# Two-layer transformer block on one core: the first layer's bias adds placed right behind the norms, its fourth turn three steps later, and the scaling of the second layer's down weights cut in four

## The chip, the cores and the metric

The kernel runs on one core of one Trainium2 chip. The metric is the device time of one execution in microseconds (us), the median of several runs. The profile is of one further execution, recorded instruction by instruction.

## The reference

`x` is 2 x 1024 tokens of width 256, in 32-bit floats. Two layers follow one another, each `x = x + attention(norm(x)) + ffn(norm(x))`:

```
xn = layernorm(x)                                   # layer 0
q, k, v = xn @ W.T + b ; qp, kp = elu(q)+1, elu(k)+1
kv = kp^T v ; z = qp . sum(kp)
attention0 = (qp @ kv) / (z + eps) @ o_w.T + o_b    # 16 heads, linear attention
ffn0 = (silu(xn @ U.T) * (xn @ G.T)) @ D.T          # ternary weights, 256 -> 1024 -> 256
xn = layernorm(x)                                   # layer 1
attention1 = softmax attention with rotary positions, 16 heads, @ out_w.T + out_b
ffn1: Walsh-Hadamard transforms around a gated FFN; its last product is scaled by Wscale_dp per output column
```

What matters here: `o_b` is a row of 256 numbers that is added to every token of `x`. `Wscale_dp` is a row of 256 numbers that scales the columns of layer 1's down weights, and a Hadamard transform of those weights over 1024 is folded into them before they are used.

## The kernel before

One function, `work_order`, writes out a single list of pieces (`put("kv_in", 3, bank)`). Each engine walks that list and issues, for every piece whose name it has a function for, its own part of it, so the list is every engine's order at once, and an engine never starts a later piece before an earlier one. Semaphores order the engines among each other.

Tokens are in four chunks of 512 (four tiles of 128). The stages around the change are these.

- **Norms.** For chunk n: `ln_stats` (VectorE statistics, then `rstd` to the power -1/2 on GpSimd), `ln_norm` (VectorE writes the normed chunk XC from X, four operations, line 1144 of the profile), `ln_turn` (TensorE transposes it, line 807; ScalarE copies the high part XH, line 1437; VectorE forms the low part XL, line 1150). X itself is only read.
- **bias.** `bias(0, c)` is one GpSimd operation, 128 x 1024, that adds `o_b` (the tile OB) to chunk c of X (line 1601). It may run once `ln_norm` has read the chunk. VectorE's later additions into X wait for it, and `load_ob1`, the load of the second layer's row into OB, waits for all four.
- **The linear attention (`attention0`, drawn as `side0`).** `kv_in(tt)` projects one tile (TensorE), VectorE adds the biases into zk and ve (lines 1215, 1216), ScalarE computes ek (lines 1454, 1456), and `kv_sum(tt)` on VectorE joins zk and ek, both in SBUF (line 1235). `kv_out` multiplies. `q0(c, m)` does the queries: QP on VectorE (line 1230), zs on ScalarE (lines 1466, 1468), the sum on GpSimd (line 1613). `att_n`, `att_t`, `att_b` apply the attention. `att_n(8)` is the first of the second batch and waits for `q0(2, 1)`.
- **Ternary weights.** `tern_abs` sums the absolute values of a 1 MB weight on ScalarE (line 1446), `tern_scale` and `tern_cut` cut it on VectorE: one operation over 2048 columns (line 1178) and two over 1024 with two SBUF inputs (line 1186). TU and TG are the up and gate weights, TD the down weights.
- **The first FFN (`main(0)`, from "half" on), woven with the rest of `side0`.** `gate`: TensorE, ScalarE's tanh (line 1508), VectorE (line 1267). `up`: TensorE, VectorE (line 1280), ScalarE's copy hh (line 1516), GpSimd's low part hl (line 1646). `down`: TensorE (line 775).
- **Second layer's down weights, on GpSimd.** `fold` multiplies the staged 128 x 2048 weights by the row WSD (line 1607). Then six `butterfly` operations of 128 x 1024 (line 1622), and `load_up` loads the next weights over them. They are put at steps of `side0`: fold at step 18, butterflies at steps 19, 22, 25, 28, 31 and 34.

Around the first norms the list before reads: `ln_norm 2`, `kv_in 1`, `kv_sum 0`, `kv_in 2`, `kv_sum 1`, `ln_turn 2`, `tern_scale 0`, `kv_in 3`, `kv_sum 2`, `ln_stats 3`, `tern_cut 0 0`, `kv_out 0`, `q0 0 0`, `ln_norm 3`, `tern_cut 0 1`, `q0 0 1`, `ln_turn 3`, `tern_abs 1`, `kv_in 4`, `kv_sum 3`, `kv_out 1`, `kv_in 5`, `kv_sum 4`, `tern_scale 1`, `kv_out 2`, `kv_in 6`, `kv_sum 5`, `tern_cut 1 0`, `kv_out 3`, `kv_in 7`, `kv_sum 6`, `tern_cut 1 1`, `kv_out 4`, `q0 1 0`, `bias 0 0`, `tern_abs 2`, `q0 1 1`, `bias 0 1`, `kv_sum 7`, `kv_out 5` to `7`, `kv_sums 0`, `bias 0 2`, `att_n 0`, `bias 0 3`, and then the FFN.

Of the kernel before, what the change touches and what calls it, by code (L numbers as in the profile page):

```python
# [8 lines left out]
ALU = mybir.AluOpType  # L9
# [40 lines left out]
class Ring:  # L50
# [5 lines left out]
    def next(self):  # L56
        self.i = (self.i + 1) % len(self.slots)
        return self.slots[self.i]
# [12 lines left out]
def work_order():  # L71
# [3 lines left out]
    def put(*piece):  # L75
        order.append(piece)
# [64 lines left out]
    def attention0():  # L141
        for tt in range(8):
            yield from kv(tt)
            if tt % 4 == 3:
                for m in range(2):
                    yield from q0(tt // 4, m)
        yield from kv_end(0)
        for h in range(4):
            yield from att_n(2 * h)
            if h:  # L150
                yield from att_b(h - 1)
            yield from att_n(2 * h + 1)
            yield from kv(8 + 2 * h)
            yield from att_t(h)
            yield from kv(9 + 2 * h)
        yield from q0(2, 0)
        yield from att_b(3)
        yield from q0(2, 1)
        yield from kv_end(1)
        for h in range(4, 8):  # L160
            yield from att_n(2 * h)
            if h > 4:
                yield from att_b(h - 1)
            yield from att_n(2 * h + 1)
            if h < 6:
                yield from q0(3, h - 4)
            else:
                yield
            yield from att_t(h)
            yield  # L170
        yield from att_b(7)
# [40 lines left out]
    def qk(c, n, count):  # L212
        put("qk", c, n, ps.next(), ps.next())
        yield
        for k in range(count):
            yield
            if k == 0:
                put("qk_join", c, n)
        put("qk_split", c, n)

    def side0():
        bf = 0
        for n, _ in enumerate(attention0()):
            if 14 <= n < 18:
                next(tn)
                if n == 17:
                    put("scales")
                    put("spread_vb")
                    put("load_wa1")
            if n == 18:  # L230
                put("fold")
            if n == 30:
                put("add_vb", ps.next())
            if n >= 18 and n % 3 == 1 and bf < 6:
                put("butterfly", bf)
                bf += 1
                if bf == 6:
                    put("load_up")
            yield
        ps.slots.append(2)  # L240
        put("prep_attn1")
        put("load_gate")
        put("difference", 0)
        yield
        for q in range(4):
            put("prep_down", q, ps.next())
            yield
            if q == 0:
                put("total", 0)
            if q == 1:  # L250
                put("difference", 1)
            if q == 3:
                put("total", 1)
        for u in range(8):
            put("prep_ug", u, ps.next())
            yield
            if u == 1:
                put("low_attn1", 0)
            if u == 5:
                put("low_attn1", 1)  # L260
        for c in (0, 1):
            for n in range(2):
                yield from qk(c, n, 4)
        put("load_m", 0)
        put("load_m", 1)
# [26 lines left out]
    next(tn)  # L292
    put("signs")
    sd0 = side0()
    next(sd0)
    next(ln0[2])
    next(sd0)
    for n in range(FIRST):
        if n < 10:
            next(tn)  # L300
        next(sd0)
        if n < 4:
            next(ln0[2 if n == 0 else 3])
        if n > 7:
            put("bias", 0, n - 8)
    put("half")
    put("load_down")
    put("load_ob1")
# [85 lines left out]
    while s < 8 * NP + LAG or any(k >= s for k in plan):  # L394
        live = s < 8 * NP
        for piece in plan.get(s, []):
            if piece[0] == "recip":
                p = piece[1]
# [23 lines left out]
        if 0 <= s - LAG < 8 * NP:  # L422
# [4 lines left out]
            elif t % 8 == 7:  # L427
                p = t // 8
# [18 lines left out]
def program(nc, x_d, wa0, tern, wa1, wo1, wf1, cols_d, bkv_d, cos_d, sin_d, had_d, mask_d, ident_d, pad_d, sel_d, wl_d, ob_d, wsd_d, y_d):  # L447
    with ExitStack() as ctx:
        base = -(-nc.sbuf_base // 32) * 32

        def sb(name, kb, shape, dt=F32):
            return nc.alloc_sbuf_tensor_at(name, shape, dt, offset=base + int(kb * KB))

        q = {n: ctx.enter_context(nc.semaphore(f"s_{n}")) for n in SEMAPHORES}
        d = {n: ctx.enter_context(nc.semaphore(f"d_{n}")) for n in DMAS}
# [46 lines left out]
        stg = [sb(f"stg{i}", 174 + 8 * i, [128, 2048]) for i in range(2)]  # L502
# [7 lines left out]
        WSD = sb("WSD", 203, [128, 256])  # L510
# [54 lines left out]
        def over_tiles(row, n):  # L565
            return row[:, :].rearrange("p (o d) -> p o d", o=1).broadcast_to([128, n, 256])
# [16 lines left out]
        def o_slots(p):  # L583
# [7 lines left out]
            return (f"oe{o}", n), (f"num{i}", done), (f"rc{o}", n), (f"rs{o}", n)  # L591

        order = work_order()
        block = ctx.enter_context(nc.Block())

# [989 lines left out]
        def _(e):  # L1585
# [14 lines left out]
                    e.wait_ge(q["ob"], 1)  # L1600
                e.tensor_tensor(xs, xs, over_tiles(OB, 4), ALU.add).then_inc(q["bx"], 1)

            def fold():
                raw = stg[0][:, :].rearrange("p (o d) -> p o d", d=256)
                e.wait_ge(d["st0"], STAGE["down"][1])
                e.wait_ge(d["wsd"], 16)
                e.tensor_tensor(raw, raw, over_tiles(WSD, 8), ALU.mult).then_inc(q["fold"], 1)

            def q0(c, m, b):
                i = 2 * c + m  # L1610
# [3 lines left out]

            def butterfly(k):
                if k == 0:
                    e.wait_ge(q["fold"], 1)
                elif k % 2 == 0:
                    e.wait_ge(q["bf"], k)
                pair = (stg[0][:, :], stg2[:, :])  # L1620
                a, z = (x.rearrange("p (o t i) -> p o t i", t=2, i=256 << k // 2) for x in (pair if k // 2 % 2 == 0 else pair[::-1]))
                e.tensor_tensor(z[:, :, k % 2, :], a[:, :, 0, :], a[:, :, 1, :], ALU.subtract if k % 2 else ALU.add).then_inc(q["bf"], 1)
# [84 lines left out]
            def low(g):  # L1707
# [3 lines left out]
                if g == 2:  # L1711
# [4 lines left out]
                    e.wait_ge(q["fill"], 2)  # L1716

            parts = {f.__name__: f for f in (ln_stats, bias, fold, q0, butterfly, low_attn1, difference, total, up, hidden, ones_v, qk_join, load_wl, out, recip, times, high, low)}
            for name, *args in order:
                if name in parts:  # L1720
# [84 lines left out]
```

## Time and profile before

| | |
|---|---|
| median of 3 runs | 731.92 us (730.15 to 731.93) |
| the profiled execution | 732.69 us, of it 730.9 us from first to last instruction |
| TensorE busy | 699.4 us (96%) |
| VectorE, ScalarE, GpSimd busy | 529.2, 432.9, 288.2 us |
| mean granted TensorE clock | 0.986 of full speed |

An operation's start and duration are on one line of the timeline, with the idle time of its engine before it and what ended that in brackets. A duration runs from issue to end, so an operation that stands waiting inside its engine shows as a long one. Neighbouring operations of an engine overlap by some hundredths of a microsecond.

### The profile page before, as it was taken

How to read it: one execution, taken by the hardware profiler on the slowest of the kernel's cores; microseconds unless marked ns; L12 is line 12 of the kernel's file. 1: busy time of each engine (PE TensorE's matmuls, PEld its weight loads, DVE VectorE, ACT ScalarE, POOL GpSimd, SP SyncE). 2: the span in 40 equal slices, each digit the busy share in tenths (PEclk: the TensorE clock that was granted, in tenths of full speed). 3: DMA queues.
4: the chain of work that ended last, by engine and by line, in shares of the span. 5: the costliest groups of instructions: out<-in, count | busy, mean ns of one | idle time of the engine just before them, and what ended most of it. 6: DMA issues, size and time to landing. Idle time of an engine off the chain costs nothing.

```text
span 730.9 us, 11063 instructions
## 1 busy us (share of the span) xinstructions
PE 699.4 (96%) x4246; PEld 441.5 (60%) x4246; DVE 529.2 (72%) x864; ACT 432.9 (59%) x592; POOL 288.2 (39%) x261
## 2 busy tenths in 40 slices
PE   7787999989998999999999999999999999999998
PEld 6576898977776888677676773333333333333445
DVE  7878875655668677678778788888886388888315
ACT  3363434446543522432332338999998999999883
POOL 2237944348665632542543431122333224332410
PEclk8999999989999999999999999999999999999999
DMA  7157001012025562423111022344443344433321
GB/s 266 55 187 231 1 1 58 1 26 91 1 87 173 167 208 87 144 70 105 59 59 35 25 67 71 126 140 160 123 143 126 100 146 146 145 94 91 105 79 58
DMA packets 25848, 74.14 MB, mean 101 GB/s; under 512 B 4620, under 2 KB 5996, under 8 KB 24964
## 3 DMA queue, kind: packets, MB, share of 16 engines
q1 hardware_dynamic: 21268, 65.37, 26.9%
q0 software_dynamic: 3808, 7.60, 3.6%
q8 instruction: 34, 0.56, 0.3%
q10 hardware_dynamic: 720, 0.48, 0.2%
q14 instruction: 18, 0.15, 0.1%
HBM read 54.54 MB, written 23.06 MB: 106 GB/s over the span
## 4 chain that ended last, share of the span: by engine, by line
PE 78%; DVE 10%; issue 5%; ACT 4%; POOL 3%; DMA 1%; DVEq 0%; ACTq 0%; POOLq 0%
PE PS L769 22%; PE PS L1038 17%; PE PS L1024 12%; PE PS L775 12%; PE PS L1007 6%; PE PS L997 5%; DVE mx L1342 1%; DVE bst L1128 1%; PE PS L903 1%; PE PS L858 1%; POOL hl L1646 1%; DVE sg L1280 1%; DVE rot L1325 1%; ACT XD L1432 1%; DMA X<-in_x 1%
## 5 line engine op out<-in xcount | busy, mean ns | idle before, releaser
L1554 ACT ACTIVATE P<-PS 128x1024 f32<-128x1024 f32 x256 | 249.0, 1024 | 30.0 <-PE PS L1024 29.7
L1349 DVE TENSOR_REDUCE mx<-PS 128x1 f32<-128x512 f32 x300 | 189.1, 682 | 32.3 <-PE PS L1007 30.6
L1342 DVE TENSOR_REDUCE mx<-PS 128x2 f32<-128x1024 f32 x106 | 124.8, 1220 | 36.6 <-PE PS L997 36.3
L1038 PE MATMUL PS<-P,VV 128*32 128x512 f32 x1024 | 136.4, 605 | 0.1
L1646 POOL TENSOR_TENSOR hl<-sg,hh 128x512 fp32r<-128x512 f32 x64 | 85.2, 1332 | 126.1 <-ACT hh L1524 75.8
L1024 PEld LDWEIGHTS PS<-QS,KS 64*128 64x128 f32 x512 | 48.4, 183 | 121.3 <-ACT P L1554 109.5
L1024 PE MATMUL PS<-QS,KS 64*128 64x512 f32 x512 | 116.4, 455 | 0.9 <-DVE mx L1342 0.6
L1007 PE MATMUL PS<-KM,QM 64*128 64x512 f32 x300 | 81.0, 395 | 0.0
L1510 ACT ACTIVATE sg<-PS,cols 128x512 f32<-128x512 f32 x32 | 22.0, 688 | 86.9 <-PE PS L769 86.9
L769 PE MATMUL PS<-XH,UGH 128*128 128x512 f32 x128 | 54.4, 425 | 3.7 <-DVE sg L1278 2.0
L769 PE MATMUL PS<-XL,UGH 128*128 128x512 f32 x128 | 50.5, 394 | 0.0
L769 PE MATMUL PS<-XH,UGL 128*128 128x512 f32 x128 | 50.0, 391 | 0.0
L1516 ACT ACTIVATE hh<-sg 128x512 fp32r<-128x512 f32 x32 | 20.1, 630 | 49.3 <-DVE sg L1280 49.3
L1655 POOL TENSOR_TENSOR sg<-sg,us 128x512 f32<-128x512 f32 x24 | 30.9, 1286 | 35.7 <-ACT us L1519 35.7
L1038 PEld LDWEIGHTS PS<-P,VV 128*32 128x32 f32 x1024 | 20.2, 108 | 39.8 <-issue 35.3
L997 PE MATMUL PS<-KM,QM 64*128 64x512 f32 x212 | 39.9, 448 | 0.8 <-DVE mx L1342 0.6
L1007 PEld LDWEIGHTS PS<-KM,QM 64*128 64x128 f32 x300 | 38.0, 185 | 3.4 <-DVE mx L1349 0.6
L775 PE MATMUL PS<-DH,hh 128*128 128x256 f32 x128 | 38.0, 297 | 0.0
L775 PE MATMUL PS<-DL,hh 128*128 128x256 f32 x128 | 36.1, 282 | 0.0
L775 PE MATMUL PS<-DH,hl 128*128 128x256 f32 x128 | 36.1, 282 | 0.0
L769 PEld LDWEIGHTS PS<-XH,UGH 128*128 128x128 f32 x128 | 24.0, 188 | 19.6 <-issue 10.8
L775 PE MATMUL PS<-TD,hh 128*128 128x256 f32 x128 | 34.0, 300 | 1.6 <-POOL hl L1646 1.6
(212 smaller groups left out, 1358.6 us busy)
## 6 DMA issues: line engine op xcount, KB each, us to landing
QM<-scr_q SPq DMA_DIRECT2D x16, 512.0 KB, 4.3
KM<-scr_k SPq DMA_DIRECT2D x16, 512.0 KB, 5.3
QS<-scr_q SPq DMA_DIRECT2D x16, 512.0 KB, 4.5
KS<-scr_k SPq DMA_DIRECT2D x16, 512.0 KB, 5.4
scr_q<-spl SPq DMA_DIRECT2D x24, 256.0 KB, 3.2
scr_k<-spl SPq DMA_DIRECT2D x24, 256.0 KB, 3.4
scr_o<-OE POOLq DMA_DIRECT2D x14, 256.0 KB, 2.8
stg<-in_tern SPq DMA_DIRECT2D x3, 1024.0 KB, 6.1
```

The costliest lines, as they stand in the source:

```text
L769: i = e.matmul(out, l, r, start=start and j == 0, stop=stop and j == len(pairs) - 1)
L775: i = e.matmul(out[:, r * 256:r * 256 + 256], l, x, start=first and r == 0 and j == 0, stop=last and j == len(pairs) - 1, skip_group_check ...
L997: e.matmul(bank[b + h], QM[p % 2][hr, qt * 128:(qt + 1) * 128], KM[p % 2][hr, chunk(half)], start=True, stop=True).then_inc(q["mt"], 1)
L1007: e.matmul(bank[b], QM[p % 2][hr, qt * 128:(qt + 1) * 128], KM[p % 2][hr, chunk(half)], start=True, stop=True).then_inc(q["mt"], 1)
L1024: i = e.matmul(bank[b + h], KS[p % 2][hr, kt * 128:(kt + 1) * 128], QS[p % 2][hr, chunk(half)], start=True, stop=True)
L1038: i = e.matmul(PS[32 * c:32 * c + 32, 7, :], v_head(8 * b + kt, 2 * j + c // 2), P[s % 4][:, chunk(c // 2 + 2 * (c % 2))], start=(kt == 0) ...
L1342: e.tensor_reduce(mx[p % 2][:, :, qt, half], PS[:, b:b + 2, :], AX.X, ALU.max).then_inc(q["mx"], 2)
L1349: e.tensor_reduce(mx[p % 2][:, h, qt, half:half + 1], bank[b], AX.X, ALU.max).then_inc(q["mx"], 1)
L1510: e.activation(s[:, :], bank[b], ACT.Silu, scale=col("wsg", m) if layer else su).then_inc(q["t"], 1)
L1554: e.activation(P[s % 4][:, half * 1024:(half + 1) * 1024], PS[:, b:b + 2, :].rearrange("p b n -> p (b n)"), ACT.Exp).then_inc(q["ex"], 1)
L1646: e.tensor_tensor(hl[f % 4][:, :], sg[f % 3][:, :], r32(hh[f % 4][:, :]), ALU.subtract).then_inc(q["hl"], 1)
L1655: e.tensor_tensor(s[:, :], s[:, :], us[f % 4][:, :], ALU.mult).then_inc(q["h"], 1)
```

## The change

The first three bias adds stand right behind `ln_norm 2` and before `kv_in 1`; the fourth stands behind `ln_norm 3`. `ln_turn 3` moves from step 3 of the loop to step 6, that is behind `kv_in 6` and `kv_sum 5`. `fold` becomes four operations over 512 columns, at steps 18 to 21 of `side0`. The six butterflies begin at step 22 instead of 19, so they stand at steps 22, 25, 28, 31, 34 and 37, and `load_up` with the last.

```diff
-            if n == 18:
-                put("fold")
+            if 18 <= n < 22:
+                put("fold", n - 18)
             if n == 30:
                 put("add_vb", ps.next())
-            if n >= 18 and n % 3 == 1 and bf < 6:
+            if n >= 22 and n % 3 == 1 and bf < 6:
                 put("butterfly", bf)
...
     next(ln0[2])
+    for c in range(3):
+        put("bias", 0, c)
     next(sd0)
     for n in range(FIRST):
         if n < 10:
             next(tn)
         next(sd0)
-        if n < 4:
+        if n in (0, 1, 2, 6):
             next(ln0[2 if n == 0 else 3])
-        if n > 7:
-            put("bias", 0, n - 8)
+        if n == 2:
+            put("bias", 0, 3)
...
-            def fold():
-                raw = stg[0][:, :].rearrange("p (o d) -> p o d", d=256)
+            def fold(k):
+
+                raw = stg[0][:, 512 * k:512 * k + 512].rearrange("p (o d) -> p o d", d=256)
                 e.wait_ge(d["st0"], STAGE["down"][1])
                 e.wait_ge(d["wsd"], 16)
-                e.tensor_tensor(raw, raw, over_tiles(WSD, 8), ALU.mult).then_inc(q["fold"], 1)
+                e.tensor_tensor(raw, raw, over_tiles(WSD, 2), ALU.mult).then_inc(q["fold"], 1)
...
-                    e.wait_ge(q["fold"], 1)
+                    e.wait_ge(q["fold"], 4)
```

## Rows read from the trace of the kernel before

**Rows 1.** The page: busy time by engine, and shares of the chain that ended last.
```profile
PE 699.4 (96%) x4246; PEld 441.5 (60%) x4246; DVE 529.2 (72%) x864; ACT 432.9 (59%) x592; POOL 288.2 (39%) x261
...
PE 78%; DVE 10%; issue 5%; ACT 4%; POOL 3%; DMA 1%; DVEq 0%; ACTq 0%; POOLq 0%
```

**Rows 2.** Two stretches: length, busy time of each engine, clock, DMA share, GB/s.
```profile
50.00:72.00 22.00, 17.19 (x84) 13.70 (x82) 16.60 (x35) 9.19 (x16) 18.16 (x10) 0.92 0.83 284
72.00:118.00 46.00, 45.82 (x279) 41.04 (x280) 34.16 (x64) 19.54 (x36) 31.54 (x17) 1.00 0.07 25
```

**Rows 3.** Timeline of TensorE: four operations that begin after idle time.
```profile
33.53 1.21 PE L807 MATMUL PS<-IDN,XC 128*128 128x128 f32 x7 [3.20 <-DVE XC L1144]
...
65.76 0.80 PE L769 MATMUL PS<-XH,TG 128*128 128x512 f32 x1 [1.96 <-DVE sg L1267]
...
72.18 0.73 PE L858 MATMUL PS<-kvb,QP 128*128 128x136 f32 x4 [1.42 <-DVE at L1247]
...
119.71 0.70 PE L858 MATMUL PS<-kvb,QP 128*128 128x136 f32 x4 [0.47 <-POOL QP L1613]
```

**Rows 4.** Timeline of GpSimd from 14 to 120 us.
```profile
15.03 2.98 POOL L1592 TENSOR_TENSOR rstd<-rstd,MINUS_HALF 128x4 f32<-128x4 f32 x1 [4.62 <-DVE rstd L1135]
...
51.10 2.40 POOL L1601 TENSOR_TENSOR X<-X,OB 128x1024 f32<-128x1024 f32 x1
...
54.70 8.10 POOL L1601 TENSOR_TENSOR X<-X,OB 128x1024 f32<-128x1024 f32 x3
62.77 3.48 POOL L1646 TENSOR_TENSOR hl<-sg,hh 128x512 fp32r<-128x512 f32 x2
...
71.32 4.60 POOL L1607 TENSOR_TENSOR stg<-stg,WSD 128x2048 f32<-128x2048 f32 x1
...
80.93 2.40 POOL L1622 TENSOR_TENSOR stg<-stg 128x1024 f32<-128x1024 f32 x1
...
116.68 1.54 POOL L1646 TENSOR_TENSOR hl<-sg,hh 128x512 fp32r<-128x512 f32 x1 [1.21 <-ACT hh L1516]
118.28 1.28 POOL L1613 TENSOR_TENSOR QP<-zs,QP 128x512 f32<-128x512 f32 x1
```

**Rows 5.** Timeline of VectorE from 57 to 82 us.
```profile
57.93 2.62 DVE L1178 TENSOR_SCALAR TD<-stg,s 128x2048 fp32r<-128x2048 f32 x1
...
62.94 2.17 DVE L1186 SCALAR_TENSOR_TENSOR TD<-stg,s,TD 128x1024 fp32r<-128x1024 f32 x1
...
66.63 1.27 DVE L1186 SCALAR_TENSOR_TENSOR TD<-stg,s,TD 128x1024 fp32r<-128x1024 f32 x1
...
81.11 2.50 DVE L1235 SCALAR_TENSOR_TENSOR zk<-zk,ek 128x256 f32<-128x256 f32 x1
```

**Rows 6.** Timeline of VectorE from 20 to 44 us.
```profile
20.91 1.37 DVE L1144 TENSOR_SCALAR XC<-X,mv,rstd 128x256 f32<-128x256 f32 x4
...
22.87 0.41 DVE L1235 SCALAR_TENSOR_TENSOR zk<-zk,ek 128x256 f32<-128x256 f32 x1
...
25.03 1.29 DVE L1150 TENSOR_TENSOR XL<-PS,XH 128x512 fp32r<-128x512 f32 x2 [0.75 <-ACT XH L1437]
...
38.11 1.29 DVE L1150 TENSOR_TENSOR XL<-PS,XH 128x512 fp32r<-128x512 f32 x2 [1.90 <-ACT XH L1437]
...
42.02 1.29 DVE L1178 TENSOR_SCALAR TG<-stg,s 128x2048 fp32r<-128x2048 f32 x1
```

**Rows 7.** Timeline of ScalarE from 24 to 39 us.
```profile
24.42 1.07 ACT L1437 ACTIVATE XH<-PS 128x512 fp32r<-128x512 f32 x2
...
38.45 1.91 ACT L1446 ACTIVATE TG<-stg 128x2048 fp32r<-128x2048 f32 x1
```

**Rows 8.** Slices of one microsecond, columns as in rows 2: the granted clock.
```profile
34.00:35.00 1.00, 1.00 (x7) 0.71 (x6) 1.00 (x3) 0.12 (x1) 0.74 (x1) 0.90 0.00 0
...
38.00:39.00 1.00, 1.00 (x6) 0.88 (x5) 0.89 (x2) 1.00 (x3) 1.00 (x1) 0.89 1.02 434
65.00:66.00 1.00, 0.24 (x1) 0.24 (x2) 1.00 (x4) 0.00 (x0) 1.00 (x1) 0.76 0.29 84
...
71.00:72.00 1.00, 0.00 (x0) 0.00 (x0) 0.93 (x4) 0.00 (x0) 1.00 (x2) 1.00 0.91 365
```

## Prediction

> **What bounds the kernel now.** I read the page first, then the chain that ended last, then the stages, then the engines' timelines. The page says TensorE: 96% busy, 78% of the chain [rows 1]. That is an average. The edits all touch work before 120 us, and there two stages differ. From 72 to 118 us TensorE is busy 45.8 of 46 us: whatever only moves GpSimd or VectorE there costs nothing. From 50 to 72 it is busy 17.2 of 22 and VectorE 16.6 [rows 2]. The idle times say who is waited for: TensorE waits 3.20 us for the fourth norm, 1.96 for VectorE's `sg`, 1.42 for VectorE's `at`, and, in the otherwise full stage, 0.47 us for GpSimd's `QP` [rows 3]. So the start is a chain through VectorE with ScalarE between, and a microsecond lost or won before the full stage reaches the end whole, since nothing behind it runs to a clock of its own.
>
> The second thing to see is that VectorE and GpSimd hold each other up. The cut of TD over 2048 columns took 2.62 us at 57.93, while three biases ran from 54.70; the same operation on TG, with GpSimd idle, took 1.29 [rows 4, 5, 6]. The cut over 1024 took 2.17 beside an `hl` and 1.27 alone. A `kv_sum` took 2.50 when a butterfly had begun 0.18 us before it, and 0.41 elsewhere [rows 4, 5, 6]. It is mutual: the `rstd` at 15.03 took 2.98 us [rows 4]. The pairs read as a queue of one: whoever comes second stands until the other's running operation ends, then gets its turn. The two `hl` at 62.77 show the turn-taking: 3.48 us for two, with the cut's 1.1 us between them [rows 4, 5].
>
> **Part 1, the first three biases early.** GpSimd is free at 15.03 + 2.98 = 18.01 us. A bias takes 2.40 us, about 2.35 from start to start [rows 4]. Biases 0 and 1 fill 18.0 to 22.7. Bias 2 needs the third norm, which ends at 20.91 + 1.37 = 22.28, so it runs from 22.7 to 25.05. `kv_sum 0`, with two SBUF inputs, comes at 22.87 [rows 6], 0.17 us after it, and waits to 25.05: **+2.2 us**. Behind it on VectorE stand `kv_in 2`, `kv_sum 1` and the third turn's XL; ScalarE's ek and XH hang on `kv_in 2`, so the 0.75 us of idle before XL at 25.03 [rows 6] gives nothing back, as XH comes from behind ek [rows 7]. VectorE is nearly unbroken from there to the fourth norm, and the whole chain moves by 2.2. Bounds: 0.9, if `kv_sum 0` wins and `kv_sum 1` at 23.87 waits instead, and 2.2. I take 2.2, since the pair 0.18 us apart lost too [rows 4, 5].
>
> The norms themselves (line 1144) I cost at nothing beside the biases: 256 columns in 0.34 us is half the rate of the cut, 2048 in 1.29 [rows 6], so this form does not run at the double rate at which the cut was held up. The Trainium skill ("VectorE: DVE Perf Modes", section "What auto-detection actually checks") would have a one-source operation with source and result in SBUF and even dimensions use both ports, and so be locked out by GpSimd; by that the norm would wait for bias 1 as well, some 1.4 us more than my sum. The trace's rate for this line speaks against it.
>
> **Part 2, the fourth bias and the fourth turn.** Today VectorE idles 1.90 us before the fourth turn's XL at 38.11 [rows 6], because transposes and XH come first. ScalarE's sum over TG begins at 38.45, right behind that XH pair (as long as the pair at 24.42, 1.07 us) [rows 7]. With the turn behind `kv_sum 5`, the sum over TG no longer waits for XH: -1.05 us, on top of +2.2. VectorE's `kv_sum 3` then meets bias 3, and `kv_sum 4` the `QP` sum behind it; the first hides under the wait for ScalarE, the second I put at +0.45 (bounds 0 and 1.3, one such operation). So the TG cut now at 42.02 starts 2.2 - 1.05 + 0.45 = 1.6 later. From there VectorE has no gap to the FFN, and XL's 1.2 us (1.29 [rows 6] less overlap) now stands in it, with 0.8 us of idle ahead, as before the third turn's XL, which follows `kv_in` and `kv_sum` in just this order: 0.75 [rows 6]. **The FFN starts 1.6 + 2.0 = 3.6 us later**; with every bound low 0.9 - 1.05 + 0 + 1.2 = 1.05, with all high 4.5.
>
> **Part 3, GpSimd free from 50 to 63 us.** The cut at 57.93 loses its wait, 2.62 - 1.29 = 1.33; the cut at 62.94 loses 2.17 - 1.27 = 0.9, as the first `hl` is then long done and the second ends as the cut begins [rows 5, 6]. Both lie on the chain through `sg` to TensorE's starts at 65.76 and 72.18 [rows 3]. **-2.2 us** (bounds -2.2, and -1.3 if the second `hl` still meets the cut).
>
> **Part 4, TensorE's clock.** It fell to its half level, 1.2 GHz, twice. It fell at 34.9 after 3.2 us of idle and came back at 38.1; it fell at 65.7 after idle 0.66 and 1.96 us with a small product between, and came back near 69. After 1.4 us of idle, at 71 to 72, it held [rows 3, 8]. Both low stretches lie where VectorE sets the pace, and cost nothing today. In the new order the up product now at 65.76 comes 2.2 earlier and at full clock; what follows it up to the wait for `at` is done 3.7 us earlier, but that wait ends only 2.2 earlier, so idle grows from 1.4 to about 3 us. The nearest row is the 3.2. If the clock falls there, its low stretch of about 3.3 us lies in the full stage, where it costs half its length: **+1.6** (bounds 0 and 1.6).
>
> **Part 5, fold and butterflies.** Four folds of 512 columns cost at most four `hl`, 4 x 1.25 = 5.0 us, for 4.60 now [rows 4]; four `hl` fit between them. All of it lies under TensorE's full stage [rows 2]; without that cover the 0.4 us would show. But the last butterfly moves to step 37, which is behind `hl` of `up 0 1 2` and ahead of the `hl` and the `QP` sum for which `att_n 8` waits. GpSimd is free at 116.68 - 1.21 = 115.47. A butterfly of 2.40 ends at 117.87, the waiting `kv_sum 15` takes 0.35, `hl` 1.25, the sum 1.28: 120.8 instead of 119.56. TensorE already waits there [rows 3, 4]: **+1.2 us** (bounds 0 and 1.25). `load_up` goes out some 9 us later and has over 40 us left. SP's queue gains: `load_ob1` no longer waits long for the biases, and nothing behind it was late.
>
> **Sum.** 3.6 - 2.2 + 1.6 + 1.2 = +4.2 us. Against the profiled execution, 732.69 + 4.2 = 736.9; the median of the runs is 0.77 lower, so 736.1. All bounds low: 1.05 - 2.2 = -1.15, or 730.8. All high: 4.5 - 1.3 + 1.6 + 1.25 = 6.05, or 738.
>
> **Rivals.**
> - *The clock holds* at the 3 us gap: +2.6, 734.5. For it: two levels, one switch, and only two falls to judge by.
> - *`kv_sum 0` slips in before bias 2*: 1.3 less, 734.8 or, with the clock held, 733.2. It is decided by 0.17 us.
> - *The early cost is absorbed.* VectorE's 1.90 us of idle at 38.11 [rows 6] takes up most of the 2.2, and TensorE's 0.47 is all that `att_n 8` shows: start +1.5, then -2.2, then +0.5: no change, 731.7. Against it: the idle goes only if TG's sum comes earlier, and that hangs on the same chain.
> - *Faster: TensorE, not VectorE, ends the chain from 33 to 49 us.* Then the moved turn fills its 3.20 us of idle [rows 3] with `kv_in 4`, the low stretch there is gone (-1.6), TG's sum gives its 1.05, and with -2.2 and +1.2 this is -3.65: 728.3. It decides from the point where the TG cut starts before about 41 us. Against it: `kv_in 4`'s bank is freed by `q0 0 0`, which hangs on VectorE.
> - *The norm is locked out too*: +1.4, 737.5. In a sentence apart, this is the rule of the Trainium skill named above.
>
> **How the numbers follow.** A measurement here tells about 0.3%, 2.2 us, from no change. The forecast at 736.1 gets 0.30 (its own range 735 to 737), the clock held 0.20, `kv_sum 0` first 0.14 (0.08 of it slower), absorbed 0.21, faster 0.13, norm locked out 0.02. Slower 0.30 + 0.20 + 0.08 + 0.02 = 0.60; same 0.06 + 0.21 = 0.27; faster 0.13. The range 731 to 738 leaves out the faster case and little above.
>
> **What would show it.** Right: `kv_sum 0` with over 2 us in it; the TG cut near 43.6 and 1.29 long; XL of the fourth turn with idle before it; gate's first tanh near 56.4 (52.8 now); the TD cut 1.29 long; a low clock just behind 72 us; `att_n 8` waiting over 1 us for `QP`. Wrong: biases beside a short `kv_sum 0`, or a TG cut at or before 42 us.

## The result, and the profile after

The changed kernel took 738.59 us (median of 4, 737.02 to 739.1) beside 731.92 (median of 4): ratio 1.0091, 95% interval 1.0070 to 1.0111. It is slower, as forecast, by 6.7 us where 4.2 was forecast, and 0.6 us above the stated range. The same kernel measured once more, in another group (run f1 below), took 737.3 beside 732.0: ratio 1.0079 (1.0059 to 1.0098). The profiled execution took 737.02 us, span 735.1: 4.3 above the profiled execution of before. That the profiled spans and the forecast both say +4.2 is luck; the part on the prediction works it out.

The first place to look is where the two traces part. In the timeline of VectorE before, lines that stand in no group above (the first four are the small operations of the piece `signs`, which prepares constants):

```profile
18.25 0.16 DVE L1163 TENSOR_SCALAR s<-cols 128x2 f32<-128x2 f32 x1
18.32 0.16 DVE L1164 TENSOR_SCALAR s16b<-cols 128x8 f32<-128x8 f32 x1
18.39 0.16 DVE L1165 TENSOR_SCALAR MINUS_QB<-cols 128x2 f32<-128x2 f32 x1
18.46 0.16 DVE L1167 TENSOR_SCALAR MASK<-MASK 128x8 f32<-128x8 f32 x1
20.24 0.42 DVE L1215 TENSOR_TENSOR zk<-PS,BKV 128x256 f32<-128x256 f32 x1 [1.61 <-PE PS L769]
...
23.20 0.42 DVE L1215 TENSOR_TENSOR zk<-PS,BKV 128x256 f32<-128x256 f32 x1
```

The timeline of VectorE after (line numbers are two higher, and three behind the fold on GpSimd):

```profile
18.04 2.14 DVE L1165 TENSOR_SCALAR s<-cols 128x2 f32<-128x2 f32 x1
20.09 0.16 DVE L1166 TENSOR_SCALAR s16b<-cols 128x8 f32<-128x8 f32 x1
20.16 2.31 DVE L1167 TENSOR_SCALAR MINUS_QB<-cols 128x2 f32<-128x2 f32 x1
22.39 0.16 DVE L1169 TENSOR_SCALAR MASK<-MASK 128x8 f32<-128x8 f32 x1
22.47 0.41 DVE L1217 TENSOR_TENSOR zk<-PS,BKV 128x256 f32<-128x256 f32 x1
...
23.13 1.37 DVE L1146 TENSOR_SCALAR XC<-X,mv,rstd 128x256 f32<-128x256 f32 x4
...
25.09 2.14 DVE L1237 SCALAR_TENSOR_TENSOR zk<-zk,ek 128x256 f32<-128x256 f32 x1
27.15 0.41 DVE L1217 TENSOR_TENSOR zk<-PS,BKV 128x256 f32<-128x256 f32 x1
...
41.09 2.17 DVE L1237 SCALAR_TENSOR_TENSOR zk<-zk,ek 128x256 f32<-128x256 f32 x1
...
45.08 1.29 DVE L1180 TENSOR_SCALAR TG<-stg,s 128x2048 fp32r<-128x2048 f32 x1
...
48.12 1.29 DVE L1152 TENSOR_TENSOR XL<-PS,XH 128x512 fp32r<-128x512 f32 x2 [0.76 <-ACT XH L1439]
...
63.04 1.29 DVE L1180 TENSOR_SCALAR TD<-stg,s 128x2048 fp32r<-128x2048 f32 x1
...
66.71 1.33 DVE L1188 SCALAR_TENSOR_TENSOR TD<-stg,s,TD 128x1024 fp32r<-128x1024 f32 x1
...
119.62 1.42 DVE L1237 SCALAR_TENSOR_TENSOR zk<-zk,ek 128x256 f32<-128x256 f32 x1
```

The timeline of GpSimd after, beside [rows 4]:

```profile
17.76 4.69 POOL L1603 TENSOR_TENSOR X<-X,OB 128x1024 f32<-128x1024 f32 x2
24.58 2.37 POOL L1603 TENSOR_TENSOR X<-X,OB 128x1024 f32<-128x1024 f32 x1 [2.13 <-DVE XC L1146]
...
118.37 2.38 POOL L1625 TENSOR_TENSOR stg<-stg 128x1024 f32<-128x1024 f32 x1
120.72 1.46 POOL L1649 TENSOR_TENSOR hl<-sg,hh 128x512 fp32r<-128x512 f32 x1
122.13 1.27 POOL L1616 TENSOR_TENSOR QP<-zs,QP 128x512 f32<-128x512 f32 x1
```

TensorE after, the two starts that answer to the last two of [rows 3], and ScalarE's first tanh, which was at 52.77 before:

```profile
75.12 0.73 PE L860 MATMUL PS<-kvb,QP 128*128 128x136 f32 x4 [2.84 <-DVE at L1249]
...
123.55 0.70 PE L860 MATMUL PS<-kvb,QP 128*128 128x136 f32 x4 [0.73 <-POOL QP L1616]
```

```profile
57.88 0.67 ACT L1510 ACTIVATE sg<-PS,s 128x512 f32<-128x512 f32 x1
```

Read as a ledger of one event after another against its old time: `kv_in 0` on VectorE +2.2 (22.47 for 20.24); `kv_in 2` +4.0 (27.15 for 23.20); the TG cut +3.1; the first tanh +5.1; `att_n 3` on TensorE +2.9; `att_n 8` +3.8; the end +4.2. The forecast had 3.6, 1.4, 4.2 (with the clock) for the tanh, `att_n 3` without the clock, and the end. Most of the distance from the forecast is made before 28 us: 4.0 at `kv_in 2`, where 2.2 was forecast, and 1.5 more than forecast at the tanh and at `att_n 3`. Two operations over two columns each, which need 0.16 us each, stand 2.14 and 2.31 us behind biases 0 and 1. The prediction charged nothing for them.

### The profile page after: what moved, and what is told of

It reads as the page before. It is cut to its first block, busy times and chain, and to the rows that moved or that the text cites. A ratio compares the mean times of both kernels' runs of the same rounds, so it can differ in the third digit from the quotient of the medians.

```text
span 735.1 us, 11069 instructions
## 1 busy us (share of the span) xinstructions
PE 702.2 (96%) x4246; PEld 443.8 (60%) x4246; DVE 534.4 (73%) x864; ACT 433.0 (59%) x592; POOL 286.8 (39%) x264
## 4 chain that ended last, share of the span: by engine, by line
PE 75%; DVE 12%; issue 5%; ACT 4%; POOL 3%; DMA 1%; DVEq 0%; ACTq 0%; POOLq 0%
PE PS L771 20%; PE PS L1040 17%; PE PS L1026 12%; PE PS L777 11%; PE PS L1009 6%; PE PS L999 5%; DVE bst L1130 1%; DVE mx L1344 1%; PE PS L905 1%; PE PS L860 1%; DVE sg L1282 1%; DVE XL L1152 1%; POOL hl L1649 1%; DVE rot L1327 1%; ACT XD L1434 1%
## 5 line engine op out<-in xcount | busy, mean ns | idle before, releaser
L1518 ACT ACTIVATE hh<-sg 128x512 fp32r<-128x512 f32 x32 | 20.2, 630 | 47.2 <-DVE sg L1282 47.2
L1040 PEld LDWEIGHTS PS<-P,VV 128*32 128x32 f32 x1024 | 20.2, 108 | 39.7 <-issue 35.2
```

The lines of the kernel that those rows point to most:

```text
L1040: i = e.matmul(PS[32 * c:32 * c + 32, 7, :], v_head(8 * b + kt, 2 * j + c // 2), P[s % 4][:, chunk(c // 2 + 2 * (c % 2))], start=(kt == 0) ...
```

## The experiments

Each kernel was run in several rounds beside the kernel before. The medians of before in the three groups (a, e and f) were 732.07, 731.67 and 732.0. A difference in us behind a ratio is that ratio times 732.

**a3, only the biases.** The kernel before with

```diff
     next(ln0[2])
+    for c in range(3):
+        put("bias", 0, c)
     next(sd0)
...
-        if n > 7:
-            put("bias", 0, n - 8)
+        if n == 2:
+            put("bias", 0, 3)
```

> The kernel before with only the four bias adds moved; turn, fold and butterflies stay. Theory A, the early biases are the loss: VectorE's two 128x2 operations of the signs piece stand 2.1 and 2.3 us and kv_sum 0 another 2.1, in all about 3.9 us before the FFN starts, and 2.2 come back at the cuts of TD: slower by 1.5 to 2.5 us. Theory B, the moved turn is the loss: within 1 us of the kernel before, or faster.

734.98 us, ratio 1.0038 (1.0023 to 1.0052): +2.8, somewhat above the 1.5 to 2.5 expected. The two small operations again took 2.14 and 2.31 us and `kv_sum 0` 2.15. In its trace `att_n 3` comes at 74.18, 2.0 later than before. Against the second measurement of the changed kernel, +5.3, the early biases alone make about half of the loss.

**a1, only the fourth turn.**

```diff
-        if n < 4:
+        if n in (0, 1, 2, 6):
             next(ln0[2 if n == 0 else 3])
```

> The kernel before with only the fourth turn moved to step 6. Theory A: the cut of TG starts about 1 us earlier, then XL with 0.8 us of idle adds 2.0: the FFN starts 1 us later, slower by 0.5 to 1.5 us. Theory B: slower by over 2 us. A third view, that TensorE sets the pace there: faster by 1 us or more.

731.99 us, ratio 1.0002 (0.9991 to 1.0013). The expected +0.5 to +1.5 is not in the median, though the interval, up to +1.0, leaves room for its lower half. The traces do show it at the stage's end: beside a2, whose early order is that of before and whose `kv_in 0` reached VectorE at the same time (19.18 for a1's 19.20), the sum kvb comes 1.08 us later. First a1, then a2, timeline of VectorE:

```profile
50.26 0.44 DVE L1224 TENSOR_TENSOR kvb<-PS,MASK 128x272 f32<-128x272 f32 x1 [0.89 <-PE PS L841]
```

```profile
49.18 0.44 DVE L1224 TENSOR_TENSOR kvb<-PS,MASK 128x272 f32<-128x272 f32 x1 [0.89 <-PE PS L841]
```

Where that microsecond goes in the median is not settled. That a1's own sum is no later than that of before (50.26 for 50.23) has another reason: `kv_in 0` came a microsecond earlier in a1's trace, of which more in the section on the prediction.

**a2, only fold and butterflies.** The kernel before with the fold and butterfly edits of the change, nothing else.

> The kernel before with only fold in four and the butterflies three steps later. Both theories: att_n 8 waits for QP behind the last butterfly, +0.9 to +1.2 us, and nothing else; from 72 to 118 us no difference. Rival: the fold in four helps or hurts the hl behind it, then over 1.5 us either way.

732.55 us, ratio 1.0010 (0.9997 to 1.0022). In its trace TensorE waits 0.75 us for `QP` at `att_n 8` (0.47 before), and `kv_sum 15` takes 1.43. The expected +0.9 to +1.2 lies inside the interval, and so does no change.

**a4, the small operations out of the way.** The changed kernel with the three operations on `cols` put earlier on VectorE; the row of MASK stays where it was.

```diff
         next(ln0[i])
+    put("signs")
     put("w0h")
...
-    put("signs")
+    put("mask_row")
...
```

`mask_row` is the last operation of `signs`, now a piece of its own.

> The changed kernel with the three small operations of the signs piece put ahead of the low part of W0, before any bias can run; the mask row stays. Theory A: they take 0.16 us each, kv_in 0 ends at its old time, kv_sum 0 still stands 2.2 us: 1.7 to 2.4 us faster than the changed kernel. Rival: kv_in 0 was late for another reason (TensorE, the loads): no difference from the changed kernel, 737 to 739 us.

736.6 us, ratio 1.0058 (1.0042 to 1.0075): 2.0 faster than the first measurement of the changed kernel, 0.7 than the second. The traces show 0.5 (first tanh 57.40 for 57.88, `att_n 3` 74.63 for 75.12), not the 1.7 to 2.4 expected. The expectation was right about the operations and wrong about what comes behind them. Timeline of VectorE, then of GpSimd, of a4:

```profile
15.01 0.16 DVE L1168 TENSOR_SCALAR MINUS_QB<-cols 128x2 f32<-128x2 f32 x1
...
18.48 2.15 DVE L1172 TENSOR_SCALAR MASK<-MASK 128x8 f32<-128x8 f32 x1
20.54 0.41 DVE L1220 TENSOR_TENSOR zk<-PS,BKV 128x256 f32<-128x256 f32 x1
...
21.21 2.88 DVE L1147 TENSOR_SCALAR XC<-X,mv,rstd 128x256 f32<-128x256 f32 x4
...
24.67 2.12 DVE L1240 SCALAR_TENSOR_TENSOR zk<-zk,ek 128x256 f32<-128x256 f32 x1
```

```profile
18.20 4.76 POOL L1606 TENSOR_TENSOR X<-X,OB 128x1024 f32<-128x1024 f32 x2
24.16 2.35 POOL L1606 TENSOR_TENSOR X<-X,OB 128x1024 f32<-128x1024 f32 x1 [1.20 <-DVE XC L1147]
```

Now the MASK row stands 2.0 us behind bias 0, all but hidden under VectorE's wait for TensorE (`kv_in 0` at 20.54 for 20.24), and the norm, 1.37 us elsewhere, takes 2.88: it stands 1.5 us behind bias 1. This is the case to which the prediction gave 0.02. In the changed kernel the norm escapes only because the small operations had already spent that time: it starts at 23.13, after bias 1 ended at 22.45.

**e1, a fuller gap.** The changed kernel with products that nobody reads, in the gap before `att_n 3`:

```diff
     weave(main(0), sd0, RATE0)
+    k = order.index(("att_n", 3, 0))
+    order.insert(k, ("busy", 12, 4))
```

> The changed kernel with 12 more products of ones with ones on TensorE, into a free bank, in the idle time ahead of att_n 3 (added work, thrown away). Theory A, the clock falls behind that gap in most executions: 1.2 to 1.8 us faster than the changed kernel, about 737.0, and the granted clock at full level from 72 to 85 us. Rival, the clock is not it and the profiled execution was only a lucky one: no difference, or 0.5 us slower if the added products get in the way.

736.54 us, ratio 1.0070 (1.0053 to 1.0087). In its trace the products fill the gap (2.94 us), no idle time is left before `att_n 3`, and the clock stays full behind it. What that is worth is judged beside f1.

**f1, the changed kernel once more, and f2, e1 with 6 products in place of 12.**

> The changed kernel itself once more, beside the others of this group. If its first four runs were fair: 738 to 739. If they were on the unlucky side of the clock's falls: 737 to 738, and then the added products of e1 bought at most 0.5 us and biases with turn (e4) are within 1.5 us of the whole change.

> The changed kernel with 6 added products before att_n 3 instead of 12, so that they end well before the gap does (the 12 took 2.94 us of 2.84). Clock theory: 0.5 to 1.5 us faster than f1, since the gap is half filled. Rival, the falls only move elsewhere: the same as f1.

f1 took 737.3 us, ratio 1.0079; f2 736.73, ratio 1.0076 (1.0057 to 1.0094). The medians of e1 and f2 lie 0.8 and 0.6 below f1, well inside the intervals: no gain is shown. The two traces of the same kernel, though, price a fall of the clock. Slices of two microseconds behind `att_n 3`, the clock third from the right: first the changed kernel, then f1, the same code.

```profile
76.00:78.00 2.00, 2.00 (x10) 1.60 (x9) 1.48 (x5) 1.01 (x2) 1.60 (x2) 1.00 0.00 0
78.00:80.00 2.00, 2.00 (x15) 1.84 (x14) 1.89 (x5) 0.92 (x3) 2.00 (x2) 1.00 0.00 0
```

```profile
76.00:78.00 2.00, 2.00 (x6) 1.51 (x6) 1.10 (x4) 0.67 (x2) 1.52 (x2) 0.50 0.00 0
78.00:80.00 2.00, 2.00 (x8) 1.59 (x7) 0.84 (x2) 0.42 (x1) 2.00 (x2) 0.71 0.00 0
```

And TensorE's starts in f1:

```profile
75.20 0.79 PE L860 MATMUL PS<-kvb,QP 128*128 128x136 f32 x4 [2.84 <-DVE at L1249]
...
125.21 0.70 PE L860 MATMUL PS<-kvb,QP 128*128 128x136 f32 x4 [0.73 <-POOL QP L1616]
```

From `att_n 3` to `att_n 8` it is 48.43 us in the one and 50.01 in the other: 1.58 for one fall, after the same 2.84 us of idle. The low stretch lasts 3.4 us. The same idle time brought the fall in one execution and not in the other. Of the seven traces with that gap of 2.84 or 2.85 us, f1, f3, a3, a4 and e2 show the fall behind it, and the changed kernel's first trace and e4 don't. In f2 the products took 1.60 us, 1.19 us of idle stayed, and the clock held. What the products save there is not visible in the medians. One reason can be read from the traces: the clock is not settled behind `att_n 8` either. Around an idle time of 1.2 to 1.3 us, between 154 and 162 us, it fell in 12 of the 14 traces, and the time from `att_n 8` to the end differs with it: 608.8 and 609.2 us in e2 and f2, where it held; 610.0 to 611.1 in the ten with a low stretch of 3.4 us; 611.2 and 611.6 in before and the changed kernel's first trace, where it was low for 6.8. So f1 is 1.66 later than that first trace at `att_n 8` and 0.1 later at the end (735.2 for 735.1). One trace for each kernel can't say how often each case comes.

**e4, biases and turn without the fold part.** The changed kernel with fold and butterflies as before.

> The changed kernel with fold and butterflies as before: biases and turn moved. If the three parts add up, 735.0 + 0.1: near 735. If biases and turn make each other worse (bias 3 runs beside kv_sum 3 only when the turn is away), 737 to 738; the fold part is then worth 0.5 to 1 us.

736.15 us, ratio 1.0064 (1.0049 to 1.0079). Its first tanh comes at 57.91 and `att_n 3` at 75.14, as in the changed kernel (57.88, 75.12); `att_n 8` at 122.68, 0.87 earlier. Biases and turn together are worth +4.7, more than a3's 2.8 and a1's 0.2, though the intervals (3.6 to 5.8; 1.7 to 3.8; -0.7 to 1.0) allow them to add up. In the traces the turn adds 0.96 us to a3 (first tanh 56.95, here 57.91); for the rest of the difference I can name no wait.

**f3, the last butterfly at its old step.**

```diff
-            if n >= 22 and n % 3 == 1 and bf < 6:
+            if n in (22, 24, 26, 28, 31, 34):
```

> The changed kernel with the butterflies at steps 22, 24, 26, 28, 31 and 34, so the last stands where the last stood before. If part 5 is right, att_n 8 waits 0.5 us instead of 0.7, its product with kv_sum 15 is not held, and 0.6 to 1.0 us come back against f1. Rival: the denser butterflies hold up other kv_sums under TensorE's full stage, which shows as idle TensorE between 80 and 115 us: no gain.

735.08 us, ratio 1.0053 (1.0036 to 1.0071), 2.2 below f1 in the medians, where 0.6 to 1.0 was expected. Its trace has the clock fall of f1, so the two can be laid side by side:

```profile
124.31 0.70 PE L860 MATMUL PS<-kvb,QP 128*128 128x136 f32 x4 [0.47 <-POOL QP L1616]
```

124.31 for 125.21: the butterfly ahead of `QP` costs 0.90 us. The wait for `QP` itself grows only from 0.47 to 0.73; the rest is the product with `kv_sum 15`, which waited 0.39 us for VectorE, and the start behind it.

**e2, the biases in VectorE's gaps.** The kernel before, with turn and fold as before, and the biases where VectorE runs only operations that were never seen to wait for GpSimd: those with an input from PSUM, and a few small ones. Two of those, in the timeline of before, beside bias 0 (51.10 to 53.50) and bias 1 (from 54.70) of [rows 4]:

```profile
52.34 0.14 DVE L1199 TENSOR_SCALAR s<-s 128x1 f32<-128x1 f32 x1
...
55.07 0.25 DVE L1243 RECIPROCAL rz<-rz 128x16 f32<-128x16 f32 x1
```

The edit:

```diff
+        if n == 3:
+            put("bias", 0, 1)
         next(sd0)
+        if n == 0:
+            put("bias", 0, 0)
...
-        if n > 7:
-            put("bias", 0, n - 8)
+        if n in (8, 9):
+            put("bias", 0, n - 6)
...
+                if layer == 0 and c == 0:
+                    e.wait_ge(q["kvk"], 2)
+                if layer == 0 and c == 1:
+                    e.wait_ge(q["tt"], 2)
```

> The kernel before with the four bias adds where VectorE needs no second port: bias 0 after kv_sum 1, bias 1 after the first cuts of TU, biases 2 and 3 in the places of the old 0 and 1. Theory A, only the lockout makes early biases dear: nothing is lost before 50 us, the cuts of TD take 1.29 and 1.3, TensorE reaches att_n 3 2.2 us earlier, but the clock now falls in the full stage (+1.6): 0 to 1 us faster than before, 731 to 732. Rival, early biases cost through something else (the semaphores, GpSimd's rstd): slower than before.

729.92 us, ratio 0.9979 (0.9968 to 0.9990): faster than both kernels, 1.5 us below before, where 0 to 1 was expected. Timelines of GpSimd, VectorE and TensorE:

```profile
23.44 2.39 POOL L1609 TENSOR_TENSOR X<-X,OB 128x1024 f32<-128x1024 f32 x1 [5.56 <-issue]
...
35.68 2.39 POOL L1609 TENSOR_TENSOR X<-X,OB 128x1024 f32<-128x1024 f32 x1
...
50.14 2.40 POOL L1609 TENSOR_TENSOR X<-X,OB 128x1024 f32<-128x1024 f32 x1
...
53.75 2.41 POOL L1609 TENSOR_TENSOR X<-X,OB 128x1024 f32<-128x1024 f32 x1
```

```profile
56.98 1.50 DVE L1182 TENSOR_SCALAR TD<-stg,s 128x2048 fp32r<-128x2048 f32 x1
```

```profile
69.27 0.73 PE L862 MATMUL PS<-kvb,QP 128*128 128x136 f32 x4 [2.85 <-DVE at L1251]
```

From the TD cut to `att_n 3` it is 12.29 us (69.27 - 56.98), 14.25 before (72.18 - 57.93). (The cut takes 1.50, not 1.29: it began while an `hl` ran.) So the good half of the change, worth 2 us at `att_n 3`, can be had without its loss. The trace has the clock's fall behind `att_n 3`, which should take most of that back; why the median gains 1.5 all the same stays open, but this trace is one of the two without the fall near 155 us. Early biases are not dear; biases beside the wrong VectorE operations are.

**e3 and f4, e2 with 12 and with 6 added products.**

> As e2, and with the 12 added products ahead of att_n 3. Theory A: both terms, 2.2 us faster than before with the clock held: 729.3 to 730.3. Rival, the clock plays no part: the same as e2.

> The kernel of e2 (biases in the gaps) with 6 added products before att_n 3. Clock theory: 0.5 to 1.5 us faster than e2, near 729. Rival, falls only move: 729.9 as e2.

730.16 us, ratio 0.9978 (0.9967 to 0.9989), and 730.1, ratio 0.9971 (0.9957 to 0.9985): neither can be told from e2.

## Why the prediction was wrong, point by point

**The direction was right, and so was most of the mechanism; one term was left out.** The failed step is in part 1, in what the first two biases cost VectorE. The prediction let them cost nothing: it costed the norms "at nothing beside the biases", because this form of operation "does not run at the double rate at which the cut was held up", and it passed over the small operations of `signs` without a word. The runs show in its place that `kv_in 0` is 2.2 us late, because two 0.16 us operations stand 2.14 and 2.31 us behind biases 0 and 1; a3, which moves only the biases, shows the same two (2.14, 2.31), and in a4, which moves these two out of the way, the MASK row (2.15) and the norm (2.88 for 1.37) wait instead. The rate was the wrong witness: operations that are slow for their size are held too.

The prediction priced a locked-out norm at 1.4 us, close to a4's 1.5, and gave it a chance of 0.02. The Trainium skill ("VectorE: DVE Perf Modes", section "What auto-detection actually checks") counts such an operation, one source and result in SBUF with even dimensions, among those that use both ports. The norm, the MASK row and the two small operations, all held, agree with it.

**That the profiled executions lie 4.2 apart, as forecast, is luck.** Part 1 had 1.8 too little; part 4 had 1.6 for a fall that this execution did not have, parts 2 and 5 each had 0.3 too much, and 0.4 came behind `att_n 8`.

**Part 1** was 2.2 us, and measured 4.0: 2.2 from the small operations and 1.7 from `kv_sum 0` (2.14 - 0.41), which waited as said though 2.2 us later, with bias 2 held back by the late norm. The early wait hides a difference between executions as well: `kv_in 0` reached VectorE at 20.24 in before's trace, but at 19.20 and 19.18 in a1 and a2, where TensorE's clock was back at full level by 16.2 us and not at 17.7; with the biases early it is 22.47 in one trace and 22.66 in a3, although TensorE's clock did not fall between 9 and 20 us in a3. All traces but a4's (20.54) fall into these groups: with the early order of before `kv_in 0` comes at 19.2 (a1, a2, e2) or at 20.2 to 20.4 (before, e3, f4), with the changed kernel's at 22.5 to 22.7 (seven traces). So at this event the change loses 2.2 or 3.3 us.

**Part 2**, forecast +1.4 on top of part 1 (3.6 - 2.2), measured +1.1 (first tanh 5.1, less 4.0). XL of the turn has 0.76 us of idle before it, as taken from the third turn; `kv_sum 3` meets bias 3 (2.17 us).

**Part 3**, forecast -2.2, measured 5.1 - 2.9 = -2.2. The cuts take 1.29 and 1.33.

**Part 4**, forecast +1.6 for a fall behind the 3 us gap: 2.84 us of idle, and 1.58 for the fall where it comes, in five of seven traces and not in the profiled execution; the rival "the clock holds" had a chance of 0.20. One reading was wrong: the clock did not fall "twice" before. It was also low from 10.9 to 17.7 us and from 154.3 to 161.1, the second time with no idle time longer than 0.64 us since 144. So neither the fall after 3.2 us nor the hold after 1.4 could be carried over safely. For the same reason a microsecond at 120 us does not reach the end whole in each execution, as the prediction has it: f1 is 5.5 behind before at `att_n 8` and 4.3 at the end.

**Part 5**, forecast +1.2, measured 0.9 (f3 against f1, and `att_n 8` +3.8 less `att_n 3` +2.9). The sign named for it, a wait of over 1 us for `QP`, did not come: the wait is 0.73, and the rest stands at the product with `kv_sum 15` (0.39) and the start behind it.

**The sum** with the measured terms is 4.0 + 1.1 - 2.2 + 0.9 = 3.8 without a fall, the difference at `att_n 8` in the profiled executions, and 5.4 with one, beside 5.3 between the medians of the second measurement, which lies inside the stated range. That agreement is not a proof: where `kv_in 0` of before comes at 19.2 the sum is a microsecond more, and the fall near 160 us shifts the end by another. The 6.7 of the first lies 1.3 above; its four executions are few, and no run here ties that excess to a cause.

## What to carry to other kernels

When GpSimd work is moved in time, list every VectorE operation in the new window that reads one tensor from SBUF and writes SBUF, or reads two from SBUF, however small: a 0.16 us operation over 128 x 2 waited as long as the GpSimd operation ran, ahead of everything queued behind it. Not all of them wait (128 x 1 and a reciprocal didn't), so look for a row of the same form. Don't infer from an operation's rate that it is exempt; if no row shows it beside GpSimd, keep the lockout as a case with real weight. The same list shows the gaps in which the moved work is free, and a wait on an existing semaphore can put it there.

## What the runs showed of the hardware that was not expected

- Single-input `TENSOR_SCALAR` operations from SBUF to SBUF that run at no visibly double rate were held by a running GpSimd operation: 128 x 256 in 0.34 us each, the four 1.37 in all, 2.88 beside a bias (a4); 128 x 2 and the strided 128 x 8, 0.16 us, 2.14 to 2.31.
- Not held beside a bias: the same operation over 128 x 1 (0.14 us at 52.34, before), a reciprocal over 128 x 16 (0.25 at 55.07, before), and an addition with one input from PSUM (`kv_in 0` of a4, 0.41 at 20.54).
- The two engines take turns with small operations too. Between biases 0 and 1 of the changed kernel VectorE got two through (the second at 20.09), and the third, at 20.16, waited for bias 1.
- After the same 2.84 us of idle TensorE's clock fell in one execution of the same code and not in another, and the fall cost 1.58 us of 50. Near 155 us the clock of before fell with no idle time over 0.64 us in the 10 us ahead of it.
